# Linear attention beside a soft decision tree on one core: value fills between keys and queries, the residual in quarters, inputs normalised a pair earlier

## The reference, cut to what matters

```python
# attention: 16 heads of 64, causal, linear; state carried along the 2048 positions
Q, K = elu(xn @ Wq + bq) + 1, elu(xn @ Wk + bk) + 1
V = xn @ Wv + bv
KV, Ks = KV + outer(k_i, v_i), Ks + k_i          # for each position i
out_i = (q_i @ KV) / (q_i . Ks + 1e-6)
attention = out @ Wo + bo
# tree: depth 8, 256 leaves
gate = sigmoid((xn @ Wq_tree.T) @ routers.T)      # 255 nodes
leaf_prob = product of g or 1 - g along each path
tree = (leaf_prob @ leaf_values) @ Wout_w.T + Wout_b
```

## Time and profile before

| | us |
|---|---|
| median of 3 runs (1218.16 to 1219.29) | 1218.85 |
| the profiled execution | 1219.74 |
| its span, first to last instruction | 1218.0 |
| PE busy (matmuls) | 1161.8, 95% |
| DVE busy | 836.1, 69% |
| POOL busy | 804.3, 66% |
| ACT busy | 681.0, 56% |

### The profile page before, as it was taken

The page is one execution under the profiler, slowest core; times in us unless marked ns, Lnnn a source line. Parts: engine busy times, 40 slices in busy tenths (PEclk is TensorE's granted clock), DMA queues, the critical chain, the costliest instruction groups (busy, mean ns, idle before and its releaser), DMA issues.

```text
span 1218.0 us, 48108 instructions
## 1 busy us (share of the span) xinstructions
PE 1161.8 (95%) x21233; PEld 996.0 (82%) x21233; DVE 836.1 (69%) x2186; ACT 681.0 (56%) x990; POOL 804.3 (66%) x951
## 2 busy tenths in 40 slices
PE   5899999999999999999999999999999999999986
PEld 4789788887878879778897888878788797888866
DVE  4775875858677585876858667585876758767482
ACT  3563674737557374673737547374673746647371
POOL 3586667667666676766667676676666667676571
PEclk9999999999999999999999999999999999999998
DMA  7143532525344252533524435252452625335251
GB/s 233 20 80 52 86 68 54 91 52 89 60 65 90 45 97 50 89 63 55 93 49 90 58 62 98 45 89 54 84 68 57 94 45 89 63 57 77 55 71 36
DMA packets 271298, 87.54 MB, mean 72 GB/s; under 512 B 250721, under 2 KB 269424, under 8 KB 271088
## 3 DMA queue, kind: packets, MB, share of 16 engines
q1 hardware_dynamic: 271088, 84.46, 39.0%
HBM read 14.43 MB, written 8.39 MB: 19 GB/s over the span
## 4 chain that ended last, share of the span: by engine, by line
PE 63%; DVE 18%; ACT 6%; DMA 5%; issue 4%; POOL 3%; SPq 1%; POOLq 0%; ACTq 0%; DVEq 0%
PE w_pair L811 17%; PE s_pair L811 11%; PE s_pair L826 9%; PE o_pair L826 9%; PE s_pair L893 5%; PE o_pair L947 4%; DVE snaps L732 4%; DVE qT L659 3%; PE o_pair L933 3%; DVE oT L697 3%; DVE v_aug L668 3%; DVE xn L645 2%; DMA k_turned<-k_planes 2%; PE kv_pair L906 2%; ACT ex L522 2%
## 5 line engine op out<-in xcount | busy, mean ns | idle before, releaser
L406 POOL TENSOR_SCALAR_AFFINE_SELECT aT<-aT 64x512 f32<-64x512 f32 x256 | 171.7, 671 | 264.6 <-ACT aT L562 254.9
L562 ACT ACTIVATE aT<-s_pair 128x512 f32<-128x512 f32 x128 | 76.5, 598 | 382.6 <-PE s_pair L893 382.6
L811 PE MATMUL w_pair<-xnT,wk 128*128 128x512 f32 x768 | 212.1, 411 | 2.2 <-ACT k_tok L535 2.2
L811 PE MATMUL s_pair<-xnT,wq 128*128 128x512 f32 x756 | 201.1, 401 | 0.6 <-DVE o_tok L709 0.3
L732 DVE TENSOR_TENSOR snaps<-kv_pair,snaps 128x65 f32<-128x65 f32 x768 | 173.4, 226 | 26.4
L467 POOL COPY k_tok<-k_turned 128x1024 uint16<-128x1024 uint16 x126 | 171.4, 1361 | 22.7 <-POOL ffn_tok L459 14.6
L811 PE MATMUL w_pair<-wv,xnT 128*128 128x512 f32 x654 | 170.0, 395 | 0.0
L525 ACT ACTIVATE ex<-ex 128x512 f32<-128x512 f32 x256 | 161.9, 633 | 8.1
L449 POOL COPY k_planes<-kT 128x1024 uint16<-128x1024 uint16 x126 | 132.7, 1053 | 49.2 <-issue 26.5
L811 PEld LDWEIGHTS w_pair<-xnT,wk 128*128 128x128 f32 x768 | 134.3, 188 | 34.4 <-ACT k_tok L535 2.7
L811 PEld LDWEIGHTS s_pair<-xnT,wq 128*128 128x128 f32 x756 | 135.1, 188 | 27.0 <-DVE o_tok L709 2.4
(11 more groups left out here) (117 smaller groups left out, 2076.6 us busy)
## 6 DMA issues: line engine op xcount, KB each, us to landing
x_in<-in_L_attn_x_dram SPq DMA_DIRECT2D x16, 256.0 KB, 3.1
x_in<-in_L_attn_x_dram SPq DMA_DIRECT2D x32, 128.0 KB, 3.2
out_dram<-y_buf SPq DMA_DIRECT2D x32, 128.0 KB, 1.7
out_dram<-y_buf SPq DMA_DIRECT2D x64, 64.0 KB, 2.3
k_turned<-k_planes SPq DMA_TRANSPOSE x126, 3.2
stage<-in_L_attn_Wv_dram SPq DMA_DIRECT2D x2, 512.0 KB, 7.8
stage<-in_L_attn_Wk_dram SPq DMA_DIRECT2D x2, 512.0 KB, 10.0
stage<-in_L_attn_Wq_dram SPq DMA_DIRECT2D x2, 512.0 KB, 12.2
```

The costliest lines, as they stand in the source:

```text
L406: pool.affine_select(out=part, in_=part, compare_op=ALU.is_ge, fill=0.0, base=0, pattern=[[0, 2 * CH], [1, D]], channel_multiplier=-1).the ...
L811: last = pe.matmul(dst, l, r, start=i == 0, stop=i == len(steps) - 1)
```

## The change

In `unit_fills` the value fills become heads, and so stand between K and Q in bank S1; xT, leaf and gate become tails, after Q in bank W1. Pair 0 keeps K, V1, Q, V1. On ACT and DVE the turned output of the unit before (L558 and L697) is now served ahead of the first fill that is neither K nor V, which is Q; `values_first` is gone. PE's waits for the mask and for the normalised output move to the middle and the last matmul of Q. POOL's residual becomes four instructions of a quarter each, in pairs 1, 3, 4 and 5. The load of block g+2 is issued in pair 6, and its inputs are normalised in pair 7 of block g, right behind the statistics; POOL computes the inverse deviation for it in the middle of the tree's levels.

```diff
     if p in (1, 2):
-        tail = [("V1", p + 1, g)]
+        head = [("V1", p + 1, g)]
         if more:
-            head = [("xT", p - 1, g + 1)]
+            tail = [("xT", p - 1, g + 1)]
+    if 3 <= p < PAIRS - 1 and more:
+        head = [("V0", p - 3, g + 1)]
     if p in (3, 4):
-        head = [("leaf", p - 3, g)]
-        if more:
-            tail = [("V0", p - 3, g + 1)]
+        tail = [("leaf", p - 3, g)]
     if p in (5, 6) and more:
-        head, tail = [("gate", p - 5, g + 1)], [("V0", p - 3, g + 1)]
+        tail = [("gate", p - 5, g + 1)]
...
# SP
-                if p == 2 and g + 2 < BLOCKS:
-                    sp.wait_ge(x_consumed, g + 1)
+                if p == 6 and g + 2 < BLOCKS:
+                    sp.wait_ge(x_consumed, CH * (g + 1))
                     load_block(g + 2)
...
# POOL
-                pool.tensor_tensor(y_buf[:, :, :], x_in[:, g % 2],
-                                   y_bias[:, 0].unsqueeze(1).to_broadcast([P, CH, hid]), ALU.add)\
-                    .then_inc(x_consumed, 1)
+                pool.tensor_tensor(y_buf[:, c], x_in[:, g % 2, c], y_bias[:, 0], ALU.add).then_inc(x_consumed, 1)
+                pool.wait_ge(x_consumed, CH * g + c + 1)
...
+            RESIDUAL_AT = (1, 3, 4, 5)
...
-                if p == 1:
-                    residual(g)
-                    pool.wait_ge(x_consumed, g + 1)
+                if p in RESIDUAL_AT:
+                    residual(g, RESIDUAL_AT.index(p))
...
                     for l in range(depth):
+                        if l == 4 and g + 2 < BLOCKS:
+
+                            inverse_deviation(g + 2)
+                            pool.wait_ge(rstd_ready, 2 * g + 6)
                         level(l, g + 1)
...
# DVE
-                if p == 0 and g + 1 < BLOCKS:
-                    normalise(g + 1)
-                fills = [name for name, _ in unit_fills(g, p, BLOCKS)]
+                if n == 0:
+                    normalise(1)
                 turned = n and by_dma(n - 1)
-                for name in values_first(fills, p):
+                for name, _ in unit_fills(g, p, BLOCKS):
                     kind, i, b = name
+                    if turned and kind not in ("K", "V0", "V1"):
+                        low_of_turned(n - 1)
+                        turned = False
...
                         if p == PAIRS - 1 and g + 2 < BLOCKS:
                             layer_norm(g + 2)
+                            normalise(g + 2)
...
# PE
-                    fill(name, head_ready if kind == "K" else normed if kind == "Q" else masked if bank == W1 and kind in ("V0", "V1") else None)
-                    if kind == "y" and i == 0:
-                        masked()
+                    if kind == "K":
+                        fill(name, at_last=inputs_ready)
+                    elif kind == "Q":
+                        fill(name, masked, normed)
+                    elif kind in ("V0", "V1"):
+                        fill(name, at_last=tail_ready)
+                    else:
+                        fill(name)
```

More of the change, by code:

```diff
@@ L408, in mask, with residual @@
                 pool.wait_ge(a_masked, 2 * n + 2)
-            def residual(g):
+            def residual(g, c):
                 if g:
@@ L670, in values @@
                    .then_inc(drained[bank_of[name]], 1)
-            def values_first(fills, p):
-                if p not in (2, PAIRS - 2):
-                    return fills
-                return [f for f in fills if f[0] not in ("Q", "V0", "V1", "oT", "kT")] + \
-                    [f for f in fills if f[0] in ("V0", "V1")] + \
-                    [f for f in fills if f[0] in ("Q", "oT", "kT")]
             def low_of_output(name):
@@ L778, in _ @@
                     elif kind == "oT":
-                        if turned:
-                            low_of_turned(n - 1)
-                            turned = False
                         low_of_output(name)
@@ L804, in until, with split_product @@
                     pe.wait_ge(signal, count)
-            def split_product(dst, lhs, rhs, tiles, at_last=None):
+            def split_product(dst, lhs, rhs, tiles, at_half=None, at_last=None):
                 steps = [s for t in range(tiles) for s in passes(lambda a, t=t: lhs(a, t), lambda a, t=t: rhs(a, t))]
                 for i, (l, r) in enumerate(steps):
+                    if at_half and i == len(steps) // 2:
+                        at_half()
                     if at_last and i == len(steps) - 1:
@@ L835, in tile_of_output, with fill @@
                 return slice(at * P, (at + 1) * P)
-            def fill(name, at_last=None):
+            def fill(name, at_half=None, at_last=None):
                 kind, i, g = name
@@ L849, in fill @@
                     last = split_product(dst, lambda a, t: xnT[:, g % 2, a, t, i * P:(i + 1) * P],
-                                         lambda a, t: wv[:, a, t, half * n:(half + 1) * n], KT_, at_last)
+                                         lambda a, t: wv[:, a, t, half * n:(half + 1) * n], KT_, at_half, at_last)
                 elif kind in ("xT", "leaf"):
@@ L1058, in head_ready, with inputs_ready @@
                             until(xn_ready, g + 1)
-                        if kind == "leaf" and i == 0:
+                        if kind == "leaf":
                             until(leaf_step, (g + 1) * LEVEL_STEPS)
+                def inputs_ready():
+                    for kind, i, g in (f for f, _ in fills):
+                        if kind == "V0" and i == 0:
+                            for t in range(KT_):
+                                until_drained(("xT", t, g))
                 def masked():
@@ L1071, in _ @@
                         normed()
-                    if kind == "V0" and i == 0:
-                        for t in range(KT_):
-                            until_drained(("xT", t, g))
                     if kind == "leaf":
-                        until(leaf_step, (g + 1) * LEVEL_STEPS)
+                        tail_ready()
                     if kind == "y" and i == 0:
```

23 lines of the change are left out of this document (11 added, 12 removed).

## The result

The change made the kernel slower by about one per cent: 1231.76 us median of 4 runs (1231.35 to 1234.34) against 1218.57 for the kernel before (4 runs, 1218.16 to 1219.29). The ratio is 1.0112, with a 95% interval of 1.0095 to 1.013. The forecast was 1227.5 us in a range of 1220 to 1243. The profiled execution of the changed kernel took 1234.34 us, with a span of 1232.5, 14.5 us longer than that of the kernel before.

A forecast was written before the change was run, and what follows sets the result against it. PE, busy 95% of the span, was taken to bound the kernel, so only its stalls could change the time. Order +5.9, last block +1.3 and port +1.5 gave +8.7 us on 1218.85: 1227.5 us, range 1220 to 1243.

The forecast's parts named there:

- the stall of 0.87 us per short unit: Pairs 1 to 4: PE has 2.90 us of work behind Q for a chain of 3.77, so stands at S.
- the chain from Q to S: From the start of Q through relu, exp and `qT` to the scores S: fixed at 3.77 us.
- The rival by which the short fill does not stall S: Pairs 1 to 4: four transposes behind Q leave S unstalled, removed stalls stay gone; 1171 us, values to 1216; 10%.
- that of a tie: Time unchanged, with a chain of 3.65 us or the last stalls smaller; 8%.
- the gains: Stalls removed per block: 0.61 us in pair 0, 0.05 in pair 1, 1.23 in pair 2, 0.52 in pair 6.
- The rare stalls: Stalls over blocks 1 to 14 beyond those of block 9; 0.78 us a block, counted as gone.
- the wait for `k_tok` in pair 2: POOL's residual delays `k_tok`, so KV waits 1.01 us; residual in quarters and values ahead of Q remove 1.23 us.
- the low half ahead of qT: `low_of_turned` before `qT` on DVE meets POOL's `k_planes`; 0 to 0.35 us a unit, taken as 0.1 a block.
- the port: Port pair shared by DVE and POOL, where the second to issue is blocked; +1.5 us over the kernel.
- The rival made of it: L697 delays `qT` throughout, 0.35 us in six pairs of 15 blocks: 1259 us, 4%; halves, 1235 to 1245, 10%.
- the last block: Pair 1 goes from 6.39 to 7.71 us with the bare chain, +1.3; pairs 2 to 4 left at 0.
- the order over 15 blocks: Units with K and V ahead of Q sum to 73.83 us a block against 73.44: +0.39 each, 5.9 in all.

The follow-up runs named there:

- The transposes made twice: Changed kernel with the four transposes of each xT and leaf fill made twice from block 1 on; 1231.97 us, ratio 1.0086 to the kernel before.
- the order alone: Kernel before with only the new order of fills and PE's waits to suit it, without `values_first`; 1244.69 us, ratio 1.0194.
- the second pair of profiles: Changed kernel and kernel before run again without an edit; changed 1231.38 to 1234.80 us, ratio 1.0106; before 1219.17 us in one run.
- the run on the two ends: Changed kernel with PE's mask wait out of the middle of Q and `oT` ahead of the tail in units 0 to 2; 1234.31 us, ratio 1.0118.
- the old order: Changed kernel with the earlier order of fills, `values_first` in pairs 2 and 6, turned output behind the fills; 1194.32 us, ratio 0.9783 to the kernel before.
- the fastest kernel: Changed kernel with new fill order only in pairs 5 and 6, `values_first` in pair 2, turned output ahead of Q only in pair 7; 1182.14 us, ratio 0.9689.

## Why the prediction was right

**Right: what bounds the kernel, and the block.** The sum of a block was 73.83 us and is 73.83, and the stall of 0.87 us per short unit was 0.89 by the S to S (7.73 to 7.78 against 6.84 to 6.88), shown as 0.70 us of idle time. The step that carried it was to lay out the chain from Q to S, 3.77 us, and to compare it with what PE has behind Q; the trace after has 3.79. The transposes made twice show the hole itself, the order alone shows that nothing else in the change is needed for it. The rival by which the short fill does not stall S is out, and so is that of a tie.

**Right: the gains.** Pair 0 gained 0.63 (0.61 forecast), pair 6 0.54 (0.52), and the wait for `k_tok` in pair 2 is gone. The rare stalls are gone too: pair 4 has 7.78 in the mean as in block 9, where it had 7.08 against 6.84.

**Wrong size: the low half ahead of qT.** I took 1.5 us for the port, and in pairs 1 to 4 it was 0: with the turned output behind, they take the same time to 0.02. L693 did begin beside `k_planes`, 0.03 us behind it, and took 1.56 us, ending 0.55 us after `k_planes`, as in the earlier trace rows. My sum had it end 0.10 us after the chain's start of `qT` and took the end of its record for the start of the next instruction, which comes 0.08 us earlier. So `qT` began only 0.03 us later than with the turned output behind (0.69 us after exp began, not 0.66), and S at the same time. The margin is that thin: nothing in the change provides for it. The Trainium skill's rule (SBUF — State Buffer, "Who interferes with whom") holds for that instruction; but in these pairs the wait fell inside slack. In the last block it did not, as shown below. The rival made of it, at 1259 or 1235 to 1245, did not come.

**Not in the prediction: pair 7.** I gave it 19.50, what it takes undisturbed before less 0.05. Before, four blocks have 20.4, which I had counted under the rare stalls; and with the turned output ahead of Q even the others gain 0.13. 19.37 in each block is 2 us less in the sum than I had, and it hides that pairs 1 to 6 came out 0.14 us a block above the forecast, of which 0.05 is pair 5, whose S before has stalled: the same 0.05 that I had given pairs 2 to 4. That the block agrees to the hundredth is luck in so far as these two cancel.

**Wrong size: block 0.** I counted it like the others, +0.4. It was +4.2, and +3.1 in the second pair of profiles. The prediction's fills are those of a unit whose output is turned by a DMA; units 0 to 2 have one fill more, `oT` in bank S1 behind the tail, which S waits for. The order alone shows it (8.39, 8.97 and 8.94 us for units 1 to 3 against 7.89, 8.13 and 7.43), and the run on the two ends takes 0.6 us of it away in each of these units. What is left over the old order (unit 3: 8.35 against 7.43) I did not take apart further; unit 4, the first without such a fill, is the forecast's 7.76 against 6.84. Block 0 also still normalises in pair 0, so the 0.61 us that I took off could not come there.

**Wrong size: the last block.** I had +1.3 for it, all in pair 1, and pair 1 gave 7.73 - 6.39 = 1.34. The whole was +2.8. Pairs 2 to 4, which I had left at 0, gave -0.16. Pair 5, of which the prediction says nothing, gave +1.08: 7.25 against 6.17. And the last S is followed by 28.8 us instead of 28.3. In pair 5 the low half meets `k_tok` on the port. PE, POOL and DVE of the changed kernel:

```profile
1202.31 1.15 PE L904 MATMUL kv_pair<-v_aug,k_tok 64*64 64x65 f32 x32 [1.32 <-POOL k_tok L468]
...
1203.66 1.08 PE L891 MATMUL s_pair<-qT,kT 64*64 64x64 f32 x32
```

```profile
1200.44 1.81 POOL L468 COPY k_tok<-k_turned 128x1024 uint16<-128x1024 uint16 x1
...
1200.38 0.68 DVE L693 TENSOR_TENSOR oT<-o_full,oT 128x512 fp32r<-128x512 f32 x1
```

L693 begins 0.06 us ahead, and `k_tok` takes 1.81 us instead of the 1.33 that it has with the turned output behind. The other 0.6 us is from KV to S: 1.35 us here and 0.75 there, at a granted clock of 0.50 from 1202 to 1204 us. The wait for the mask in the middle of Q shows 0.54 us of idle time, but it costs nothing by itself: with the turned output behind it shows 0.55, and pair 5 takes 6.17 all the same. In the run on the two ends Q has no such wait, and L693 begins 0.34 us behind `k_tok`, as ACT had to wait 0.26 us for the DMA of the turned output. DVE and POOL there:

```profile
1200.22 1.49 DVE L693 TENSOR_TENSOR oT<-o_full,oT 128x512 fp32r<-128x512 f32 x1
...
1199.88 1.34 POOL L468 COPY k_tok<-k_turned 128x1024 uint16<-128x1024 uint16 x1
```

Here `qT` is what comes late, and pair 5 takes 6.57. So it is the turned output ahead of Q that costs pair 5 its 1.08 us, on the port and by the clock: in this unit the port's theory holds.

**Not in the prediction: the start.** I did not look at it, +2.0 us. On DVE the low half of `wk` (L283, L282 before) took 3.44 us in the changed kernel and 1.22 in the kernel before. First the changed kernel, DVE, POOL and PE:

```profile
23.50 3.44 DVE L283 TENSOR_TENSOR wk<-stage,wk 128x1024 fp32r<-128x1024 f32 x1
...
23.47 2.39 POOL L283 TENSOR_TENSOR wk<-stage,wk 128x1024 fp32r<-128x1024 f32 x1 [1.20 <-ACT wk L515]
...
27.00 2.54 PE L809 MATMUL w_pair<-xnT,wk 128*128 128x512 f32 x6 [1.89 <-DVE wk L283]
```

And the kernel before, DVE and POOL:

```profile
24.70 1.22 DVE L282 TENSOR_TENSOR wk<-stage,wk 128x1024 fp32r<-128x1024 f32 x1
...
24.85 3.35 POOL L282 TENSOR_TENSOR wk<-stage,wk 128x1024 fp32r<-128x1024 f32 x1 [2.00 <-ACT wk L511]
```

Before, DVE comes 0.15 us ahead of POOL; after, 0.03 us behind, and PE waits 1.89 us for it. The race is lost in both profiles of the changed kernel, in that of the two ends and in that of the fastest kernel (S of unit 1 at 46.99 to 47.27), and won in all others (44.03 to 44.98). Among these is the kernel with the transposes made twice, whose program is that of the changed kernel until its first xT fill in unit 1: it had 44.31. So it can fall either way with the same instructions. The changed kernel's other three runs, at 1231.35 to 1231.87 us, lie 2.5 to 3.0 us under the profiled one, and two of its repetition 3.3 to 3.4 (1231.38 and 1231.47 against 1234.80); with the two ends, though, two of three do not (1234.26 and 1234.52 against 1234.36). That suggests that these 2 us belong to the profiled execution rather than to the change; it is not shown, as the other runs have no profile. Whether the change makes losing likelier, no run here tells.

In sum: the median rose by 13.2 us, where +8.7 was forecast. Of the span the forecast was +8.7 us, of which +5.9 for the order over 15 blocks, +1.3 for the last block and +1.5 for the port. The trace has +5.5 for 14 blocks, +4.2 for block 0, +2.8 for the last block and +2.0 for the start. The middle was right (+5.5 forecast for 14 blocks), and the ends, which the prediction did not go through unit by unit, made the difference.

## What to carry to other kernels

On an engine that works in the order of its program, what stands behind a product is the cover of its drain chain: before moving a fill, measure the chain from the fill's start to the matmul that needs it (3.8 us here), and count what is left behind it (2.9). A reordering can be hidden among edits that each gain; here it turned -2.2% into +1.1%, so try each part alone, and put the fill that is longest behind the one with the chain, as in pairs 5 and 6. Units at the ends of a loop, which have other fills, deserve a count of their own.

## What the runs showed of the hardware that I had not expected

**Which of two engines starts first decides which of them pays.** DVE's `wk` above took 1.22 us 0.15 ahead of POOL's and 3.44 us 0.03 behind it; POOL's took 3.35 and 2.39. The same holds in unit 0 of the kernel before, where the four parts of `xn` on DVE meet POOL's `k_tok`; first the profile shown ahead, then the second one, DVE and POOL:

```profile
49.26 1.79 DVE L645 TENSOR_SCALAR xn<-x_in,mean_var,rstd 128x256 f32<-128x256 f32 x4
...
50.71 1.55 POOL L467 COPY k_tok<-k_turned 128x1024 uint16<-128x1024 uint16 x1 [0.78 <-POOL aT L406]
```

```profile
48.82 2.84 DVE L645 TENSOR_SCALAR xn<-x_in,mean_var,rstd 128x256 f32<-128x256 f32 x4
...
50.10 1.40 POOL L467 COPY k_tok<-k_turned 128x1024 uint16<-128x1024 uint16 x1 [0.60 <-POOL aT L406]
```

One program, two executions, 1.05 us apart in this group and 1.03 in the unit. `k_tok` begins 1.45 us into the four parts in the first and 1.28 in the second. With 0.45 us for a part (an estimate, 1.79 / 4), the last part had begun in the first and had not in the second. A single profile can't tell such a microsecond from an effect of a change.

**Two pauses of PE came with a lower clock, and others did not.** The windows of the changed kernel at the start and in the last block (columns: us, then busy us and instructions of PE, PEld, DVE, ACT and POOL, granted clock, DMA share, GB/s):

```profile
24.00:28.00 4.00, 2.11 (x8) 1.38 (x7) 4.00 (x4) 2.03 (x3) 3.75 (x2) 0.94 0.75 236
28.00:32.00 4.00, 4.00 (x13) 3.14 (x12) 3.24 (x3) 1.32 (x2) 2.85 (x2) 0.64 0.02 8
...
1200.00:1204.00 4.00, 2.44 (x81) 2.02 (x82) 1.78 (x4) 1.32 (x2) 2.92 (x3) 0.71 0.42 72
```

PE had waited 1.89 us for `wk`, until 27.00. The granted clock was then 0.64 over 28 to 32 us, and 0.50, which is 1.2 GHz, from 28 to 30; six matmuls of 512 columns took 2.54 us there and take 1.56 at full clock. In the last block, around the 1.32 us at KV, it was 0.71, and S took 1.08 us instead of 0.65. From 32 to 1200 us it was 1.00, though PE stood 0.70 us in 56 units there, 1.14 us at 1174 and 1.49 us at 42.6. What tells these pauses apart, no run here shows.
